# The operand that two comparison lines read lies in PSUM instead of SBUF, in a graph-network kernel

## The chip, the cores and the metric

The kernel runs on one core of one Trainium2 chip. The metric is the device time of that core in microseconds (us): the median of several executions.

## The reference

Four graph layers over 6250 nodes with 96 features each and 106250 edges, each followed by a residual sum and a layer norm. Cut to what matters here:

```
# layer 0, twice: an edge's message, the maximum over the edges that end in a node
msg = x[src] @ W_msg + edge_attr @ W_edge
agg = segment_max(msg, dst);  x' = leaky_relu(agg + x @ W_root + b)
# layer 1: weights from a small network on the edge, sum over the edges
agg = segment_sum(w(edge_attr) * x[src], dst)
# layer 2: two hops over the normalised adjacency; layer 3: one more
h = segment_sum(norm[:, None] * h[src], dst)
```

## The kernel before

**Two halves.** Layers 0 and 1 need x[src] for every edge: three passes over the edges (p = 0, 1, 2). Edges are sorted by destination and cut into 832 tiles of 128 edges; four tiles are a quarter (208 in a pass). Layers 2 and 3 are done with a dense adjacency matrix, 50 blocks of 128 nodes by 6272, which is counted up on the chip during passes 1 and 2 and written to memory, and then read and multiplied three times.

**The gathers.** GpSimd (POOL) issues one indirect DMA for each tile (line 851, `gath<-table,ids`), 832 in a pass, one after the other. It waits at a pass's start for the node table, and within a pass only that the work on the quarter eight back has let go of the buffer (`s_turn`, signalled by TensorE's line 1093; `s_msg` of VectorE's line 2343 in pass 2). A gather moves 128 rows of 384 bytes; its descriptors are made by software on GpSimd.

**A step of passes 0 and 1** works on one quarter. TensorE turns the gathered rows (L1090) and adds the edge's part (L1093); VectorE scans them (L2161, `scan`); TensorE turns back (L1107); VectorE makes the one-hots of the band (L2166); TensorE adds up (L1133). In pass 0 VectorE also makes the one-hots of a histogram (L1826, L1828): these compare with `span_ps`, a table of 0 to 127 as 4-byte numbers in PSUM bank 7. In pass 2 the step has a product (L2343) in place of the scan.

**The adjacency's windows.** In steps 8 to 207 of pass 1 and 0 to 199 of pass 2, VectorE builds one-hots for two windows of the adjacency: `window_hots` writes `hot_key` (128x392, bf16, L2190) and `hot_src` (128x128, bf16, L2192), two of each for a window, so four pairs a step and 1600 pairs in all. Each compares a table that is the same for all (`iota_key` of 392 int16 numbers, `iota_b` of 128 bf16 numbers, both in SBUF) with one number for each partition, a column of `key_t` in SBUF. TensorE multiplies them (L1161) into PSUM bank 6, and ScalarE takes the counts out (L1587). The window one-hots stand ahead of the same step's scan in VectorE's order; there are four buffers of each (`h`).

Every engine runs its instructions in the order written; semaphores join them. Between the test at the start (`falls_ps`) and the dense half, nothing but VectorE's `span_ps` is written to bank 7 in this path.

Of the kernel before, what the change touches and what calls it, by code (L numbers as in the profile page):

```python
# [24 lines left out]
BF16 = mybir.dt.bfloat16  # L25
I32 = mybir.dt.int32
I16 = mybir.dt.int16
ALU = mybir.AluOpType
# [7 lines left out]
P = 128  # L36
# [32 lines left out]
KEYS = HI * WINDOW  # L69
# [62 lines left out]
def gnn_kernel(nc, x_nodes, x_t, src_t, dst_t, dst_now, dst_before, ea17_t, ea32_t, ea17_rows, ea32_rows,  # L132
# [43 lines left out]
    with ctx:  # L176
        def sb(name, shape, dt=F32, at=None):
            return (at or ctx).enter_context(nc.sbuf_tensor(name, shape, dt))
# [42 lines left out]
        iota_b = sb("iota_b", [P, P], BF16)  # L221
        strays = sb("strays", [P, 2])
        rel_end = sb("rel_end", [P, TILES])
        iota_key = sb("iota_key", [P, KEYS], I16)
# [21 lines left out]
        with ExitStack() as sparse:  # L246
# [32 lines left out]
            with ExitStack() as of_fast:  # L279
# [4 lines left out]
                key_t = sb("key_t", [P, 2, KEY_TILES, NT * WINDOWS], at=of_fast)  # L284
# [5 lines left out]
                hot_key = sb("hot_key", [P, 4, KEY_TILES, KEYS], BF16, of_fast)  # L290
                hot_src = sb("hot_src", [P, 4, KEY_TILES, P], BF16, of_fast)
# [4 lines left out]
        banks = ctx.enter_context(nc.psum_tensor("banks", [P, 8, 512], F32))  # L296
# [22 lines left out]
        key_t_ps = [banks[:, b, 0:2 * KEY_TILES * GATHERED] for b in (6, 1)]  # L319
        window_ps = banks[:, 6, 0:KEYS]  # L320
        span_ps = banks[:, 7, 0:P]
        before_ps = banks[:, 0, 0:2 * NT]
        hid1_ps = banks[0:D, 0, :]
        wide_w_ps = [banks[:, b, 0:QT * D] for b in (4, 5)]
# [156 lines left out]
        def over_groups(eng, *stages):  # L481


            def step(i, b, known):
                for stage, lag in stages:
                    g = 2 * i + b - lag if known else None
                    if not known or 0 <= g < GROUPS:
                        stage(i + (b - lag) // 2, (b - lag) % 2, known and g < 2)
            for s in range(4):
                step(s // 2, s % 2, True)  # L490
            with eng.Fori(2, GPAIRS) as i:
                step(i, 0, False)
                step(i, 1, False)
            for s in range(GROUPS, GROUPS + max(lag for _, lag in stages)):
                step(s // 2, s % 2, True)
# [41 lines left out]
        def over_units(eng, peeled, *stages):  # L537

            def step(i, b, known):
                for stage, lag in stages:  # L540
                    t = 2 * i + b - lag if known else None
                    if not known or 0 <= t < UNITS:
                        stage(i + (b - lag) // 2, (b - lag) % 2, 1 if t == UNITS - 1 else 3)
            for s in range(peeled):
                step(s // 2, s % 2, True)
            with eng.Fori(peeled // 2, TRIOS // 2) as i:
                step(i, 0, False)
                step(i, 1, False)
            for s in range(TRIOS, UNITS + max(lag for _, lag in stages)):
                step(s // 2, s % 2, True)  # L550
# [1228 lines left out]
        def _(ve):  # L1779
# [353 lines left out]
            with ve.Else():  # L2133
# [3 lines left out]
                ve.tensor_tensor(rel_end[:, :], ids[:, 0, :], reaches()[:, 0:TILES], ALU.subtract)  # L2137
                ve.wait_ge(s_y[0], GROUPS)
                ve.tensor_copy(span_ps, iota_b[:, :])
                ve.wait_ge(s_next, 32)  # L2140
                ve.drain()
                ve.tensor_tensor(part[:, :].bitcast(F32), ids[:, 0, :], part[:, :], ALU.is_equal)
# [39 lines left out]
                def window_hots(p, i, k):  # L2182

                    for j in (0, 1):
                        n = WINDOWS * BUILT * (p - 1) + WINDOWS * i + 2 * k + j
                        h = 2 * (k % 2) + j
                        if n >= 4:
                            ve.wait_ge(s_window_mm, n - 3)
                        for a in range(KEY_TILES):
                            ve.tensor_scalar(hot_key[:, h, a, :], iota_key[:, :], key_t[:, 0, a, bass.ds(n, 1)],  # L2190
                                             None, ALU.is_equal)
                            last = ve.tensor_scalar(hot_src[:, h, a, :], iota_b[:, 0:P], key_t[:, 1, a, bass.ds(n, 1)],  # L2192
                                                    None, ALU.is_equal)
                        last.then_inc(s_window_hot, 1)

# [114 lines left out]
                for p in range(2):  # L2310
                    if p == 1:
                        degrees()
                        ve.wait_ge(s_x, 16)
                    for s in range(QUARTERS + TAIL):
                        for i, k in windows_at(p, s, 0):
                            window_hots(p, i, k)
                        if s < QUARTERS:
                            scan_quarter(p, s)
                        if 2 <= s < QUARTERS + 2:
                            hots_of_ends(p, s - 2)  # L2320
                        if p == 0 and s < QUARTERS:
                            one_hots(s)
                        for g in bands_at(p, s, 1):
                            rectify(p, g)
                        if p == 1:
                            for g in bands_at(p, s, 3):
                                add_rows(g)
                            for g in bands_at(p, s, 5):
                                factors_of(p, g)
                            if s == 2:  # L2330
                                key_places()
                        if s == KEYS_AT:
                            (make_keys if p == 0 else take_keys)()
# [16 lines left out]
                for s in range(QUARTERS + TAIL):  # L2350
                    if s + 1 < QUARTERS:
                        message(s + 1)
                    for i, k in windows_at(2, s, 0):
                        window_hots(2, i, k)
                    for g in bands_at(2, s, 2):
                        add_sums(g)
                    for g in bands_at(2, s, 4):
                        factors_of(2, g)
                    for g in bands_at(2, s, 6):
                        parts_of(g)  # L2360
# [111 lines left out]
```

## Time and profile before

| | us |
|---|---|
| median of 3 runs (4173.12 to 4182.38) | 4178.61 |
| the profiled execution, its time | 4181.7 |
| its span, first to last instruction | 4179.9 |
| PE busy | 3225.5 (77%) |
| POOL busy | 2408.2 (58%) |
| DVE busy | 2313.7 (55%) |
| ACT busy | 893.1 (21%) |

Engines: PE is TensorE, DVE VectorE, ACT ScalarE, POOL GpSimd. Busy shares are over the whole span, and they mix the gather passes (the first gather starts at 40.6 us, the last at 3255.4 us) with the dense half after them, in which POOL does nothing. In a row of groups, "x784 | 765.3, 976" is 784 instructions, 765.3 us busy together, 976 ns a piece; behind the next bar stands the idle time of the engine ahead of them, with what ended it. In a timeline row the first two numbers are start and duration in us.

### The profile page before, as it was taken

The page shows a single profiled execution, that of the slowest core. Times are in us where ns is not written, and L with a number is a line of the kernel's source. Part 1 is how long each engine was busy: PE and PEld are TensorE (multiplying, and loading weights), DVE is VectorE, ACT ScalarE, POOL GpSimd, SP SyncE. Part 2 cuts the span into 40 slices and gives each one's busy share as a digit, 9 for nine tenths or more (in the row PEclk, how much of TensorE's full clock was granted, in tenths as well). Part 3 has the DMA queues.
Part 4 walks back from the last instruction along what each step waited for, and adds up shares of the span by engine and source line. Part 5 has one row for each costly group of instructions (what it writes and reads, how often), then busy time and mean ns, then how long its engine had stood idle before and what let it go on. Part 6 is the DMA issues. An engine that isn't in the chain of part 4 may idle for free.

```text
span 4179.9 us, 64017 instructions
## 1 busy us (share of the span) xinstructions
PE 3225.5 (77%) x23472; PEld 2587.8 (62%) x23472; DVE 2313.7 (55%) x6280; ACT 893.1 (21%) x1914; POOL 2408.2 (58%) x2520
## 2 busy tenths in 40 slices
PE   3767666666667776777777778888778899999999
PEld 2545445555445454545545555555555899999999
DVE  3867677676567676767664565556655222223111
ACT  0111111111123232333333333333333000011011
POOL 4777777777677777777766777777777100000000
PEclk9888888898888898989898998889888899999999
DMA  5433333333344444444433333333333677777775
GB/s 154 120 84 73 84 84 75 83 73 86 68 110 115 118 114 120 108 120 110 118 89 89 101 89 93 88 93 90 99 93 83 225 268 268 266 271 263 263 260 208
DMA packets 173212, 555.29 MB, mean 133 GB/s; under 512 B 75512, under 2 KB 81115, under 8 KB 149146
## 3 DMA queue, kind: packets, MB, share of 16 engines
q1 hardware_dynamic: 62384, 335.45, 24.7%
q0 software_dynamic: 80432, 124.45, 14.3%
q10 hardware_dynamic: 30138, 92.02, 5.8%
q8 instruction: 153, 2.51, 0.3%
q14 instruction: 105, 0.86, 0.1%
HBM read 455.05 MB, written 96.37 MB: 132 GB/s over the span
## 4 chain that ended last, share of the span: by engine, by line
POOL 50%; PE 26%; issue 18%; DMA 4%; DVE 1%; ACTq 0%; ACT 0%; DVEq 0%; POOLq 0%; SPq 0%
POOL gath L851 50%; PE banks L1365 21%; DMA gath<-table,ids 2%; PE banks L1093 1%; DMA w_l<-in_w_l 1%; PE banks L1133 1%; PE banks L1090 1%; DMA gath<-in_dst_now 0%; PE banks L1107 0%; DMA key_got<-key_runs,key_ix 0%; PE banks L1161 0%; DVE hot_lo L1826 0%; DVE scan L2161 0%; PE banks L1349 0%; PE banks L877 0%
## 5 line engine op out<-in xcount | busy, mean ns | idle before, releaser
L851 POOL DMA_INDIRECT gath<-table,ids x2496 | 2396.9, 960 | 814.2 <-issue 750.2
L1365 PE MATMUL banks<-r_parts,adj_in 128*128 128x288 bf16 x7203 | 889.8, 286 | 6.9 <-DMA adj_in<-adjacency 5.7
L1365 PEld LDWEIGHTS banks<-r_parts,adj_in 128*128 128x128 bf16 x7203 | 883.2, 142 | 8.9 <-issue 5.9
L2161 DVE TENSOR_TENSOR_SCAN scan<-keep_of,scan,banks 96x512 f32<-96x512 bf16 x414 | 526.9, 1273 | 562.3 <-PE banks L1093 561.1
L1090 PE MATMUL banks<-ident,gath 128*96 128x128 f32 x1664 | 290.7, 303 | 634.6 <-issue 287.9
L1133 PE MATMUL banks<-back 128*96 128x104 f32 (+11 forms) x6000 | 688.3, 263 | 17.9 <-ACT back L1577 8.1
L1133 PEld LDWEIGHTS banks<-back 128*96 128x96 f32 x6000 | 648.5, 177 | 70.3 <-issue 41.3
L1090 PEld LDWEIGHTS banks<-ident,gath 128*96 128x96 f32 x1664 | 189.9, 137 | 700.3 <-issue 356.4
L1587 ACT ACTIVATE adj<-banks 128x392 bf16<-128x392 f32 x800 | 395.4, 494 | 1026.5 <-PE banks L1161 1024.6
L1161 PE MATMUL banks<-hot_key,hot_src 128*128 128x392 bf16 x1600 | 430.7, 353 | 215.0 <-DVE hot_src L2192 199.2
L2190 DVE TENSOR_SCALAR hot_key<-iota_key,key_t 128x392 bf16<-128x392 int16 x1600 | 546.7, 342 | 11.8 <-PE banks L1161 5.9
L1093 PE MATMUL banks<-ea_of,w_edge_of 128*96 128x512 f32 x832 | 493.5, 679 | 0.0
L1161 PEld LDWEIGHTS banks<-hot_key,hot_src 128*128 128x128 bf16 x1600 | 147.2, 105 | 528.9 <-DVE hot_src L2192 314.4
L2192 DVE TENSOR_SCALAR hot_src<-iota_b,key_t 128x128 bf16<-128x128 bf16 x1600 | 401.9, 251 | 0.0
L1577 ACT ACTIVATE back<-banks 128x384 f32<-128x384 f32 x416 | 203.1, 488 | 913.1 <-PE banks L1107 899.9
L2343 DVE TENSOR_TENSOR back<-banks,gath 128x384 f32<-128x384 f32 x208 | 115.5, 555 | 390.8 <-DMA gath<-table,ids 370.6
L1107 PEld LDWEIGHTS banks<-ident,scan 96*128 96x128 f32 x1664 | 208.4, 155 | 174.3 <-issue 151.8
L1300 PEld LDWEIGHTS banks<-w_edge_out,hid 97*128 97x128 f32 x1664 | 242.9, 214 | 28.8 <-issue 15.6
L2385 DVE TENSOR_REDUCE v<-banks 128x288 f32<-128x864 f32 (+1 forms) x34 | 34.8, 1022 | 404.1 <-PE banks L1365 404.0
L1300 PE MATMUL banks<-w_edge_out,hid 97*128 97x96 f32 x1664 | 241.2, 294 | 5.7 <-DVE back L2343 5.7
L1292 PE MATMUL banks<-ea_of,w_edge_of 128*96 128x512 f32 x416 | 236.5, 653 | 8.1 <-DMA ea_of<-in_ea_t 7.3
L2166 DVE TENSOR_TENSOR back<-rel_end,banks 128x416 f32<-128x416 f32 x416 | 231.7, 557 | 2.6 <-PE banks L1133 2.6
(167 smaller groups left out, 2042.5 us busy)
## 6 DMA issues: line engine op xcount, KB each, us to landing
adj_in<-adjacency SPq DMA_DIRECT2D x147, 1568.0 KB, 6.5
adjacency<-adj ACTq DMA_DIRECT2D x100, 784.0 KB, 5.8
gath<-table,ids POOLq DMA_INDIRECT x2496
ea_of<-in_ea_t SPq DMA_DIRECT2D x78, 512.0 KB
keep_of<-keep_max_d SPq DMA_DIRECT2D x52, 768.0 KB, 13.1
key_runs<-key_lines ACTq DMA_DIRECT2D x4, 896.0 KB
table<-x_sb SPq DMA_DIRECT2D x10, 240.0 KB, 4.3
back<-in_x_t SPq DMA_DIRECT2D x12, 192.0 KB
```

What stands on the lines that cost most here:

```text
L851: pool.indirect_dma_start(gath[:, b, t, :], None, tables[p][:, :], bass.IndirectOffsetOnAxis(ap=ids[:, 1, n:n + 1], axis=0),).then_inc(s_g ...
L1090: pe.matmul(turn_ps[q % 2][:, t * P:(t + 1) * P], gath[:, k // 4, QT * (k % 4) + t, :], ident[:, :], start=t == 0, stop=False, is_transpos ...
L1093: pe.matmul(turn_ps[q % 2], weights(p), columns, start=False, stop=True, skip_group_check=True).then_inc(s_turn, 1)
L1133: m = pe.matmul(band_ps[g % 2][:, at:at + n], rows_in[:, q % 2, t * D:(t + 1) * D], hot_dst[:, q % 2, t, first:first + n], start=False, st ...
L1161: m = pe.matmul(window_ps, hot_src[:, 2 * (k % 2) + j, a, :], hot_key[:, 2 * (k % 2) + j, a, :], start=a == 0, stop=a == KEY_TILES - 1)
L1292: pe.matmul(hid1_ps, weights(2), columns, start=True, stop=True).then_inc(s_hid_ps, 1)
L1300: m = pe.matmul(wide_w_ps[q % 2][:, t * D:(t + 1) * D], hid[:, q % 2, t * P:(t + 1) * P], W["edge_out"][:, :], start=True, stop=True)
L1365: m = pe.matmul(sum_ps[:, u, j, :], adj_in[:, a, :, h], r_parts[:, n % 2, h, :, :].rearrange("p k f -> p (k f)"), start=h == 0, stop=h == ...
L1587: act.activation(adj[:, half, at:at + WINDOW, :].rearrange("p d h -> p (d h)"), window_ps, ACT.Copy)\
L2161: ve.tensor_tensor_scan(scan[0:D, b, at:at + Q], keep_of[:, i % 2, CHUNK * b + at:CHUNK * b + at + Q], turn_ps[q % 2], start, ALU.min, ALU ...
L2190: ve.tensor_scalar(hot_key[:, h, a, :], iota_key[:, :], key_t[:, 0, a, bass.ds(n, 1)], None, ALU.is_equal)
L2192: last = ve.tensor_scalar(hot_src[:, h, a, :], iota_b[:, 0:P], key_t[:, 1, a, bass.ds(n, 1)], None, ALU.is_equal)
```

## The change

Two more tables in PSUM bank 7, behind `span_ps`: `key_places_ps`, the 392 int16 numbers of `iota_key`, and `src_places_ps`, the 128 bf16 numbers of `iota_b`. They are written once, as 4-byte words by a shift of 0 places (196 and 64 words). The two comparisons of `window_hots` read these in place of the tables in SBUF. Outputs, the numbers compared, counts and order stay.

```diff
+        key_places_ps = banks[:, 7, P:P + KEYS // 2].bitcast(I16)
+        src_places_ps = banks[:, 7, P + KEYS // 2:P + KEYS // 2 + P // 2].bitcast(BF16)
...
                 ve.tensor_copy(span_ps, iota_b[:, :])
+                ve.tensor_scalar(banks[:, 7, P:P + KEYS // 2].bitcast(I32), iota_key[:, :].bitcast(I32), 0, None, ALU.arith_shift_right)
+                ve.tensor_scalar(banks[:, 7, P + KEYS // 2:P + KEYS // 2 + P // 2].bitcast(I32), iota_b[:, :].bitcast(I32), 0, None, ALU.arith_shift_right)
                 ve.wait_ge(s_next, 32)
...
                         for a in range(KEY_TILES):
-                            ve.tensor_scalar(hot_key[:, h, a, :], iota_key[:, :], key_t[:, 0, a, bass.ds(n, 1)],
+                            ve.tensor_scalar(hot_key[:, h, a, :], key_places_ps, key_t[:, 0, a, bass.ds(n, 1)],
                                              None, ALU.is_equal)
-                            last = ve.tensor_scalar(hot_src[:, h, a, :], iota_b[:, 0:P], key_t[:, 1, a, bass.ds(n, 1)],
+                            last = ve.tensor_scalar(hot_src[:, h, a, :], src_places_ps, key_t[:, 1, a, bass.ds(n, 1)],
                                                     None, ALU.is_equal)
```

VectorE's queue with the change, at the end of its setup for the sparse half (`banks` is PSUM; `part` and `rel_end` are prepared for the band one-hots, and the first scan of pass 0 follows):

```order
L2139 TENSOR_TENSOR rel_end<-ids,agg 128x832
L2141 CAST banks<-iota_b 128x128
L2142 TENSOR_SCALAR banks<-iota_key 128x196
L2143 TENSOR_SCALAR banks<-iota_b 128x64
L2146 TENSOR_TENSOR part<-ids,part 128x832
L2148 SCALAR_TENSOR_TENSOR rel_end<-part,rel_end 128x832
L2165 SCALAR_TENSOR_TENSOR scan<-keep_of,banks 96x512
```

The rows of L2142 and L2143 are new there; they stand ahead of the wait for the row of `part`, and nothing else has moved (line numbers are four higher from there on). On no other engine does an instruction come, go or move.

## Rows read from the trace of the kernel before

**Rows 1.** The chain that ended last: shares of the span by engine.

```profile
POOL 50%; PE 26%; issue 18%; DMA 4%; DVE 1%; ACTq 0%; ACT 0%; DVEq 0%; POOLq 0%; SPq 0%
```

**Rows 2.** Busy us (instructions) in four stretches: PE, PEld, DVE, ACT, POOL; clock, DMA.

```profile
300.00:1090.00 790.00, 529.56 (x4436) 400.82 (x4437) 553.39 (x958) 86.88 (x176) 597.45 (x633) 0.86 0.34 78
1181.00:2184.20 1003.20, 728.66 (x4879) 508.63 (x4877) 703.83 (x2121) 310.82 (x693) 764.61 (x784) 0.90 0.42 113
2205.00:3225.10 1020.10, 801.07 (x4852) 575.61 (x4851) 602.79 (x2176) 359.20 (x715) 774.48 (x807) 0.88 0.33 92
3225.10:3256.40 31.30, 24.97 (x151) 20.48 (x150) 7.08 (x15) 4.30 (x8) 23.63 (x26) 0.76 0.26 65
```

**Rows 3.** POOL's groups: 300:1090, 1112:1181, 1181:2184.2, 2205:3225.1, 3225.1:3256.5, in this order.

```profile
L851 POOL DMA_INDIRECT gath<-table,ids x633 | 598.2, 945 | 192.9 <-issue 190.4 <-PE banks L1093 2.4
...
L851 POOL DMA_INDIRECT gath<-table,ids x49 | 46.3, 945 | 30.9 <-DMA table<-y 16.3 <-issue 14.3 <-DVE key_ix L2227 0.3
...
L851 POOL DMA_INDIRECT gath<-table,ids x784 | 765.3, 976 | 238.9 <-issue 235.5 <-PE banks L1093 3.4
...
L851 POOL DMA_INDIRECT gath<-table,ids x807 | 774.5, 960 | 266.4 <-issue 243.1 <-DMA table<-node 20.8 <-DVE back L2343 2.4
...
L851 POOL DMA_INDIRECT gath<-table,ids x26 | 24.6, 945 | 7.9 <-issue 7.9
```

**Rows 4.** Who POOL waited for, 1181:2184.2: us, times, longest.

```profile
POOL gath L851 <- issue: 235.5, 773, 0.3
```

**Rows 5.** Timeline of POOL and VectorE near the end of pass 1.

```profile
2180.65 0.94 POOL L851 DMA_INDIRECT gath<-table,ids  x1 [0.30 <-issue]
...
2181.16 0.52 DVE L2190 TENSOR_SCALAR hot_key<-iota_key,key_t 128x392 bf16<-128x392 int16 x1
...
2181.60 0.23 DVE L2192 TENSOR_SCALAR hot_src<-iota_b,key_t 128x128 bf16<-128x128 bf16 x1
...
2181.76 0.31 DVE L2190 TENSOR_SCALAR hot_key<-iota_key,key_t 128x392 bf16<-128x392 int16 x1
...
2181.90 1.07 POOL L851 DMA_INDIRECT gath<-table,ids  x1 [0.30 <-issue]
...
2183.28 0.94 POOL L851 DMA_INDIRECT gath<-table,ids  x1 [0.30 <-issue]
```

**Rows 6.** VectorE's groups of pass 0, 300:1090.

```profile
L2161 DVE TENSOR_TENSOR_SCAN scan<-keep_of,scan,banks 96x512 f32<-96x512 bf16 x159 | 202.4, 1273 | 221.2 <-PE banks L1093 221.0
L1826 DVE TENSOR_TENSOR hot_lo<-lo_dst,banks 128x512 bf16<-128x512 bf16 x158 | 107.2, 679 | 15.6 <-PE banks L1149 14.6 <-issue 0.4
```

**Rows 7.** VectorE's groups: two of 1181:2184.2 (pass 1), one of 2205:3225.1 (pass 2).

```profile
L2190 DVE TENSOR_SCALAR hot_key<-iota_key,key_t 128x392 bf16<-128x392 int16 x796 | 265.7, 334 | 11.8 <-PE banks L1161 5.9 <-ACT key_t L1610 5.5
L2161 DVE TENSOR_TENSOR_SCAN scan<-keep_of,scan,banks 96x512 f32<-96x512 bf16 x199 | 253.2, 1273 | 289.0 <-PE banks L1093 288.1
...
L1872 DVE CAST r_parts<-sq 128x384 bf16<-128x384 f32 x11 | 4.2, 379 | 0.8
```

**Rows 8.** Timeline of VectorE in pass 1: comparisons back to back.

```profile
1402.17 0.24 DVE L2192 TENSOR_SCALAR hot_src<-iota_b,key_t 128x128 bf16<-128x128 bf16 x1
1402.33 0.31 DVE L2190 TENSOR_SCALAR hot_key<-iota_key,key_t 128x392 bf16<-128x392 int16 x1
1402.56 0.31 DVE L2192 TENSOR_SCALAR hot_src<-iota_b,key_t 128x128 bf16<-128x128 bf16 x1
1402.72 0.31 DVE L2190 TENSOR_SCALAR hot_key<-iota_key,key_t 128x392 bf16<-128x392 int16 x1
```

**Rows 9.** Timeline of VectorE in pass 0: comparisons with the table in PSUM.

```profile
600.98 0.68 DVE L1826 TENSOR_TENSOR hot_lo<-lo_dst,banks 128x512 bf16<-128x512 bf16 x1
601.58 0.35 DVE L1828 TENSOR_TENSOR hot_hi<-hi_dst,banks 128x200 bf16<-128x200 bf16 x1
601.85 0.68 DVE L1826 TENSOR_TENSOR hot_lo<-lo_src,banks 128x512 bf16<-128x512 bf16 x1
```

**Rows 10.** Timeline of VectorE behind the place of the two new writes.

```profile
72.87 1.02 DVE L2142 TENSOR_TENSOR part<-ids,part 128x832 f32<-128x832 int32 x1 [26.54 <-DMA part<-ids]
```

## The prediction

> **What bounds the kernel now.** I read the chain that ended last first, then the busy times by stretch, then GpSimd's own groups in each stretch. The chain puts half of the span on POOL, and another 18% on "issue" [rows 1], which is time between instructions with nothing awaited. The only POOL work of any size is the gathers of L851, so the passes' length is their number times their period. That POOL is the bound, and not a queue that waits for others, is seen in what ended its idle time in pass 1: "issue" 235.5 us in 773 gaps, none over 0.3 us [rows 4]. Nobody holds it back there. Each gather is followed by a constant gap of 0.30 us [rows 5], and the next starts.
>
> So the question is how long one gather occupies POOL, and the groups by stretch answer it [rows 3]. In pass 0 a gather takes 945 ns (633 of them). At the start of pass 1, before the window one-hots begin, it takes 945. With the window one-hots running it takes 976 in pass 1 (784) and 960 in pass 2 (807). In pass 2's last steps, when they have ended, it takes 945 again. The same instruction, the same bytes, and its length changes exactly with the work of L2190 and L2192.
>
> The timeline shows how [rows 5]. The gather that starts at 2180.65 ends at 2181.59. A `hot_key` that starts inside it, at 2181.16, takes 0.52 us where 0.31 is usual, and so ends with the gather. The next gather starts at 2181.90, while a `hot_key` is under way, and takes 1.07 us where 0.94 is usual. Each makes the other wait: the two engines want something that only one can have at a time.
>
> Not every VectorE instruction does that. In pass 0 VectorE is busy 553 of 790 us [rows 2], as full as in pass 1 (704 of 1003), with scans and with one-hots that read `span_ps` in PSUM [rows 6], and the gathers stay at 945. These have one input in SBUF and one in PSUM; the scan even has a number per partition from SBUF besides.
>
> **The change part by part.**
>
> *The waiting of the gathers, removed.* Pass 1: 784 x (976 - 945) ns = 24.3 us. Pass 2: 807 x (960 - 945) ns = 12.1 us. From the second I take off what is not the comparisons' own: that stretch has 11 casts of L1872 [rows 7] and as many of L1868, SBUF to SBUF like the comparisons, and they will go on disturbing gathers. I estimate 0.1 us each, 2 us. That leaves 24 + 10 = 34 us. It goes straight to the end: POOL waits for nobody, pass 2 starts from pass 1's last gather, and the dense half starts from pass 2's.
>
> The whole 34 us is given back only if the comparisons no longer contend at all when their table lies in PSUM. The trace has no one-input comparison of 2-byte numbers in PSUM. The bounds are 0 (it contends as before) and 34 us. The nearest rows are those of pass 0 [rows 6], and they stand at no contention whatever: 945 ns. I take 34.
>
> The Trainium skill says the same as a mechanism. "SBUF — State Buffer", section "Who interferes with whom", has GpSimd share one pair of ports with VectorE as an exclusive lock that a `tensor_scalar` takes in its two-port modes, and descriptor making on GpSimd stands still meanwhile. "VectorE: DVE Perf Modes", section "Why PSUM operands drop a tier", has a PSUM operand exclude the two-port modes. The trace agrees with the first as far as it goes (0.52 and 1.07 us in rows 5); the second no run has shown yet.
>
> *The comparisons' own time, added.* Back to back, a `hot_key` holds the engine 0.23 us (1402.33 to 1402.56) and a `hot_src` 0.16 (1402.17 to 1402.33) [rows 8]: 0.07 us for 264 more numbers, 0.265 ns a number, and 0.13 us fixed. A pair takes 0.39. Comparisons with the PSUM table in pass 0 take 0.60 for 512 and 0.27 for 200 [rows 9]: 1.06 ns a number and 0.06 fixed. Those are two-input and read 4-byte numbers. What the new form costs is bounded from these:
> - least: half the present rate (0.53 ns a number) with the fixed part of rows 9: 0.06 + 0.21 and 0.06 + 0.07 = 0.40, nothing added;
> - most: the rate of rows 9 with the present fixed part: 0.13 + 0.42 and 0.13 + 0.14 = 0.82, that is +0.43 a pair;
> - taken: half the present rate and the present fixed part, 0.34 + 0.20 = 0.54, +0.15 a pair. The present rate is four times that of rows 9; no row lies between. I take the middle step because the inputs stay 2-byte numbers side by side, which those of rows 9 are not, while the memory becomes that of rows 9.
>
> Does that matter? VectorE has room: in pass 1 it idles 1003.2 - 703.8 = 299 us and in pass 2 417 us [rows 2]. Taken over 796 pairs, +0.15 is 119 us of the 299. The cover is the wait of the scan for TensorE, 289 us in that stretch [rows 7], which is a wait for gathers to land. Without that cover every pair would cost its 0.15 us, 240 us in all. A late scan delays POOL only once it is late by some seven quarters of 5 us, since the gathers run that far ahead. So: 0.
>
> The Trainium skill has a rule against this change. Its table in "VectorE: DVE Perf Modes", section on the TRN2 errata, charges 58 cycles fixed for an SBUF source and 120 for one in PSUM, at 0.96 GHz some 65 ns more per instruction, on top of the lower rate. That would make a pair 0.54 + 0.13 = 0.67 and add 223 of 299 us in pass 1: still hidden, the same time. The trace points the other way, a fixed 0.06 us with a PSUM operand against 0.13 [rows 8, 9].
>
> *The two writes, added.* At 196 and 64 words they cost under 0.6 us together by the rate and fixed part of rows 9. They stand ahead of a wait of 26.54 us for a transfer [rows 10]: hidden, 0. If that cover were gone: 0.6 us.
>
> *The tails.* When a pass's last gather lands, the engines run dry behind it. Pass 2 has no windows in its last eight steps. In pass 1 the last block of comparisons starts right behind a step's band one-hots and has the 4 us in which the gather is under way; 0.6 us more disappears in it.
>
> Sum: 4181.7 - 34 = 4147.7 for the profiled execution, which is 3.1 us above the median of the runs: 4178.6 - 34 = **4145 us**.
>
> **The rivals.**
>
> *A. It still contends.* The result still goes to SBUF and the number per partition still comes from there; if one of these is what is fought over, nothing changes: 4178.6. For it: no row has this very form. Against it: `hot_lo` writes 512 bf16 numbers to SBUF, the scan reads a number per partition, and pass 0 has 945 ns. Chance 0.08. A middle case, where the longer instruction contends on some of its way, gives half: 4162, chance 0.08.
>
> *B. VectorE becomes the bound (slower).* If the new form takes one number per clock as in rows 9 and keeps its fixed part, a pair takes 0.82. In pass 1 a step holds four pairs: VectorE's 703.8/199 = 3.54 us a step become 3.54 + 4 x 0.43 = 5.26, and a step lasts 5.04 now. Pass 1 would grow by 199 x 0.22 = 44 us, and pass 2, where VectorE has 417 us spare against 800 x 0.43 = 344, would still give 10: 4178.6 + 44 - 10 = 4213. It decides from +0.376 us a pair (299/796) on, and somewhat sooner as the scan's waits can't all be filled. For it: every PSUM row of the trace has that rate. Against it: they are all 4-byte and two-input. Chance 0.07.
>
> **How the numbers follow.** The forecast, the gathers back to 945 ns in both passes and VectorE hidden, has 0.77; with the executions' spread of some 5 us and the 2 us estimate its own range is 4138 to 4153. The middle case lies at 4153 to 4170, A at 4170 to 4187, B at 4190 to 4220. Leaving out A, B and the far part of the middle case leaves out less than 2 in 10: **4137 to 4165**. 0.2% is 8.4 us, about what a measurement of this kernel can tell from no change. Faster by more than that: 0.77 and most of the middle case, 0.84. Within it: 0.09. Slower: 0.07.
>
> **What would show it.** Right: the groups of L851 at 945 to 948 ns in pass 1 and about 947 in pass 2, the gaps still 0.30, the last gather starting some 34 us before 3255 us; `hot_key` no longer 0.52 anywhere beside a gather, pairs 0.5 to 0.6 us apart, VectorE's busy time in pass 1 up by about a tenth of the stretch. Wrong in the first step: gathers of 960 and 976 ns still there. Wrong in the second: POOL's idle time ended by PE L1093 or by a VectorE line with whole microseconds, and the scan's wait for PE gone. The dense half should not change: any difference behind the last gather is none of this argument.

## The result, and the profile after

The changed kernel takes 4143.59 us (median of 4 runs, 4141.57 to 4145.7), the kernel before 4180.49 beside it: a ratio of 0.9918, 95% interval 0.9906 to 0.993. That is 37 us less, at a forecast of 4145 and 34 less. Of the executions told of below, one was far slower than the others of its kernel (only `hot_src` from PSUM: 5133.3 us at a granted clock of 0.56 against 0.90) and is in no median and no ratio.

First the page's chain of waits of the changed kernel, then POOL's groups in the same five kinds of stretch as in [rows 3]: pass 0; pass 1 before the windows; pass 1 beside them; pass 2 beside them; the last steps of pass 2.

```profile
POOL 49%; PE 26%; issue 18%; DMA 4%; DVE 2%; SPq 0%; DVEq 0%; ACT 0%; ACTq 0%; POOLq 0%
```

```profile
L853 POOL DMA_INDIRECT gath<-table,ids x632 | 597.5, 945 | 192.6 <-issue 190.8 <-PE banks L1095 1.8
...
L853 POOL DMA_INDIRECT gath<-table,ids x47 | 44.4, 944 | 30.5 <-DMA table<-y 16.5 <-issue 14.0
...
L853 POOL DMA_INDIRECT gath<-table,ids x786 | 743.1, 945 | 239.5 <-issue 233.4 <-PE banks L1095 6.1
...
L853 POOL DMA_INDIRECT gath<-table,ids x808 | 764.0, 946 | 268.4 <-issue 242.9 <-DMA table<-node 22.4 <-DVE back L2347 3.0
...
L853 POOL DMA_INDIRECT gath<-table,ids x25 | 23.6, 943 | 7.6 <-issue 7.6
```

The third and fourth rows had 976 and 960 ns. Now every stretch has the 943 to 946 ns of a gather that nobody disturbs, and POOL is still the bound (49 + 18% of the chain). The gaps have not grown: 239.5 us for 786 gathers is 0.30 us each.

VectorE in pass 1 beside the windows, by groups, to be read beside [rows 7]; then the engines' busy us (PE, PEld, DVE, ACT, POOL) in four stretches, the last of them the dense half:

```profile
L2194 DVE TENSOR_SCALAR hot_key<-banks,key_t 128x392 bf16<-128x392 int16 x797 | 326.3, 409 | 12.1 <-PE banks L1163 6.5 <-ACT key_t L1612 5.4
L2165 DVE TENSOR_TENSOR_SCAN scan<-keep_of,scan,banks 96x512 f32<-96x512 bf16 x199 | 252.8, 1270 | 190.8 <-PE banks L1095 190.3
L2196 DVE TENSOR_SCALAR hot_src<-banks,key_t 128x128 bf16<-128x128 bf16 x796 | 216.3, 272 | 0.0
```

```profile
300.00:1090.00 790.00, 542.18 (x4464) 410.49 (x4465) 553.84 (x957) 87.17 (x176) 597.38 (x632) 0.84 0.34 78
1174.00:2156.70 982.70, 739.89 (x4891) 518.96 (x4890) 781.51 (x2123) 312.52 (x693) 742.60 (x786) 0.88 0.43 115
2179.20:3187.80 1008.60, 791.61 (x4854) 569.27 (x4854) 673.45 (x2178) 360.77 (x715) 762.67 (x808) 0.89 0.33 93
3219.00:4141.80 922.80, 903.84 (x7360) 900.96 (x7360) 211.90 (x597) 76.21 (x211) 0.00 (x0) 0.99 0.72 259
```

VectorE works longer for the same result (781.5 us in a stretch that is 20 us shorter, where it was 703.8), and pays with idle time: the scan's wait for PE fell from 289 to 190 us. The last gather's stretch ends at 3219.0 us where it ended at 3256.4, 37 us earlier, and the dense half takes its 923 us as before (4179.9 - 3256.4 = 923.5).

A piece of the timeline, POOL and VectorE in pass 1, shows what no longer happens:

```profile
1395.84 0.94 POOL L853 DMA_INDIRECT gath<-table,ids  x1 [0.30 <-issue]
1395.91 0.41 DVE L2194 TENSOR_SCALAR hot_key<-banks,key_t 128x392 bf16<-128x392 int16 x1
1396.24 0.27 DVE L2196 TENSOR_SCALAR hot_src<-banks,key_t 128x128 bf16<-128x128 bf16 x1
1396.43 0.41 DVE L2194 TENSOR_SCALAR hot_key<-banks,key_t 128x392 bf16<-128x392 int16 x1
1396.76 0.27 DVE L2196 TENSOR_SCALAR hot_src<-banks,key_t 128x128 bf16<-128x128 bf16 x1
1396.95 0.41 DVE L2194 TENSOR_SCALAR hot_key<-banks,key_t 128x392 bf16<-128x392 int16 x1
1397.08 0.94 POOL L853 DMA_INDIRECT gath<-table,ids  x1 [0.30 <-issue]
```

Comparisons start at different moments of a gather, and neither is longer for it. They also give the new form's price: 0.33 us for `hot_key` (1396.43 to 1396.76) and 0.19 for `hot_src` (1396.24 to 1396.43). That is 0.14 us for 264 numbers, 0.53 ns a number, and 0.12 us fixed, where [rows 8] gave 0.13.

### The profile page after: what moved, and what is told of

Read it like the earlier page. It is cut to its first block, busy times and chain, and to the rows that moved or that the text cites. A ratio compares the mean times of both kernels' runs of the same rounds, so it can differ in the third digit from the quotient of the medians.

```text
span 4141.8 us, 64019 instructions
## 1 busy us (share of the span) xinstructions
PE 3235.8 (78%) x23472; PEld 2597.4 (63%) x23472; DVE 2460.8 (59%) x6282; ACT 895.3 (22%) x1914; POOL 2373.2 (57%) x2520
## 4 chain that ended last, share of the span: by engine, by line
POOL 49%; PE 26%; issue 18%; DMA 4%; DVE 2%; SPq 0%; DVEq 0%; ACT 0%; ACTq 0%; POOLq 0%
POOL gath L853 49%; PE banks L1367 21%; DMA gath<-table,ids 3%; PE banks L1095 1%; PE banks L1135 1%; PE banks L1092 1%; DMA ea_of<-in_ea_t 1%; PE banks L1163 1%; DMA gath<-in_dst_now 0%; PE banks L1109 0%; PE banks L1351 0%; SPq L681 0%; DVE hot_key L2194 0%; DVE back L2347 0%; POOL key_got L863 0%
## 5 line engine op out<-in xcount | busy, mean ns | idle before, releaser
L853 POOL DMA_INDIRECT gath<-table,ids x2496 | 2361.9, 946 | 811.5 <-issue 748.2
L2194 DVE TENSOR_SCALAR hot_key<-banks,key_t 128x392 bf16<-128x392 int16 x1600 | 656.8, 411 | 12.1 <-PE banks L1163 6.5
L2196 DVE TENSOR_SCALAR hot_src<-banks,key_t 128x128 bf16<-128x128 bf16 x1600 | 436.8, 273 | 0.0
L1109 PE MATMUL banks<-ident,scan 96*128 96x96 f32 x1664 | 231.6, 267 | 3.9 <-ACT back L1579 3.9
```

The source lines that it names most:

```text
L853: pool.indirect_dma_start(gath[:, b, t, :], None, tables[p][:, :], bass.IndirectOffsetOnAxis(ap=ids[:, 1, n:n + 1], axis=0),).then_inc(s_g ...
L1109: m = pe.transpose(back1_ps[:, t * D:(t + 1) * D], scan[0:D, k // 4, at + t * P:at + (t + 1) * P], ident[0:D, 0:D])
L2194: ve.tensor_scalar(hot_key[:, h, a, :], key_places_ps, key_t[:, 0, a, bass.ds(n, 1)], None, ALU.is_equal)
L2196: last = ve.tensor_scalar(hot_src[:, h, a, :], src_places_ps, key_t[:, 1, a, bass.ds(n, 1)], None, ALU.is_equal)
```

## The experiments

Twelve experiments ran on eleven kernels (the drain alone twice); three of them, on another chip, are told of further down only. Each ratio is to the kernel before as it ran beside (medians of 4177 to 4180 us). The last two columns are the mean length of a gather beside the windows, from POOL's groups.

| kernel | us | ratio to before, 95% | pass 1, ns | pass 2, ns |
|---|---|---|---|---|
| before [rows 3] | 4179 | | 976 | 960 |
| changed | 4143.6 | 0.9906 to 0.993 | 945 | 946 |
| only hot_key from PSUM | 4148.8 | 0.9906 to 0.994 | 947 | 947 |
| only hot_src from PSUM | 4171.1 | 0.9973 to 0.9992 | 963 | 961 |
| 4-byte tables in SBUF | 4178.1 | 0.9988 to 1.0007 | 982 | 954 |
| changed, histogram from SBUF | 4322.7 | 1.0313 to 1.0358 | 947 | 947 |
| changed, all comparisons twice | 4496.4 | 1.0741 to 1.0787 | 945 | 944 |
| changed, hot_src twice | 4151.0 | 0.9916 to 0.9954 | 947 | 947 |
| changed, hot_key twice | 4239.0 | 1.0132 to 1.0169 | 948 | 947 |
| before, hot_key twice, drain | 4158.5 | 0.9943 to 0.9973 | 952 | 954 |
| before, drain alone | 4164.5 | 0.9959 to 0.998 | 956 | 957 |

### Each part alone

```diff
# e1: only hot_key reads PSUM
-  last = ve.tensor_scalar(hot_src[:, h, a, :], src_places_ps, key_t[:, 1, a, bass.ds(n, 1)], ...
+  last = ve.tensor_scalar(hot_src[:, h, a, :], iota_b[:, 0:P], key_t[:, 1, a, bass.ds(n, 1)], ...
# e2: only hot_src reads PSUM
-  ve.tensor_scalar(hot_key[:, h, a, :], key_places_ps, key_t[:, 0, a, bass.ds(n, 1)], ...
+  ve.tensor_scalar(hot_key[:, h, a, :], iota_key[:, :], key_t[:, 0, a, bass.ds(n, 1)], ...
```

> One part alone: hot_key reads its table from PSUM, hot_src still from SBUF. Theory (a one-input comparison that runs SBUF to SBUF and a gather's descriptor making keep each other waiting, each for as long as the other holds): hot_key no longer disturbs, hot_src does as before. It is the shorter of the two (0.16 us of a pair's 0.39), so a third or less of the 31 and 15 ns stays: gathers of some 955 ns in pass 1 and 949 in pass 2, the whole about 4155 us. Rival (each VectorE instruction that reads a table in SBUF costs the same, whatever its length): half stays, 960 and 953 ns, about 4162 us. Rival (only VectorE's total load counts): no step at all between the two kernels, since the load rose with the change.

> The other part alone: hot_src from PSUM, hot_key from SBUF. Theory: the longer instruction still disturbs, two thirds or more of the excess stay: 967 ns or more in pass 1, 955 or more in pass 2, about 4168 us. Rival of equal shares: 960 and 953 ns, 4162 us. Together with the run before, the savings of the two should add to about 36 us if they act independently.

POOL's groups beside the windows of pass 1 and of pass 2, with only `hot_key` in PSUM:

```profile
L853 POOL DMA_INDIRECT gath<-table,ids x786 | 744.1, 947 | 239.5 <-issue 234.4 <-PE banks L1095 5.2
...
L853 POOL DMA_INDIRECT gath<-table,ids x807 | 763.9, 947 | 266.4 <-issue 243.8 <-DMA table<-node 20.8 <-DVE back L2347 1.8
```

and with only `hot_src` in PSUM:

```profile
L853 POOL DMA_INDIRECT gath<-table,ids x786 | 756.8, 963 | 239.6 <-issue 234.4 <-PE banks L1095 5.2
...
L853 POOL DMA_INDIRECT gath<-table,ids x808 | 776.2, 961 | 266.7 <-issue 244.4 <-DMA table<-node 20.8 <-DVE back L2347 1.5
```

`hot_key` carries nearly all: 30 us of the 36 come with it alone, 8 with `hot_src` alone. In the two profiled executions 5.5 us of what separates "only hot_key" from the changed kernel lie ahead of pass 1 (its first gather starts at 1113.0 us against 1107.5), so the gathers are the better measure: 947 ns against 945 and 946. Equal shares per instruction are out, and so is the idea that VectorE's load sets it. My third for `hot_src` alone was too much (947 ns measured in both passes, 955 and 949 expected). Nor do the shares add up pass by pass: with only `hot_src` moved, pass 1 fell from 976 to 963 ns, further than the 967 or more that I had expected, and pass 2 did not fall at all.

### The same length of comparison, the other memory

```diff
# before, with the tables as 4-byte numbers in SBUF
+  ve.tensor_copy(wide_tables[:, 0:KEYS], iota_key[:, :])
+  ve.tensor_copy(wide_tables[:, KEYS:KEYS + P], iota_b[:, :])
...
-  ve.tensor_scalar(hot_key[:, h, a, :], iota_key[:, :], key_t[:, 0, a, bass.ds(n, 1)], ...
+  ve.tensor_scalar(hot_key[:, h, a, :], wide_tables[:, 0:KEYS], key_t[:, 0, a, bass.ds(n, 1)], ...
```

(`hot_src` likewise.)

> Both tables stay in SBUF but as 4-byte numbers, so that a comparison should take as long as with the PSUM table (hot_key 0.33 us and hot_src 0.19 us start to start) and VectorE's load is that of the changed kernel; only the memory differs. Theory (the place of the input decides): the gathers stay disturbed, and somewhat more than before as the comparisons last longer: 976 ns or up to 990 in pass 1, 960 to 970 in pass 2, the whole 4178 to 4195 us. Rival (it is the fast form, four 2-byte numbers a cycle, that disturbs, and any slower form would have done): gathers back to 945 ns, the whole about 4144 us.

POOL beside the windows of pass 1 and of pass 2; then the durations (least, median, most, in ns) of `hot_key` in this kernel and in the changed one:

```profile
L853 POOL DMA_INDIRECT gath<-table,ids x784 | 770.0, 982 | 238.9 <-issue 234.7 <-PE banks L1095 4.3
...
L853 POOL DMA_INDIRECT gath<-table,ids x808 | 770.7, 954 | 268.4 <-issue 242.9 <-DMA table<-node 22.4 <-DVE back L2349 3.0
```

```profile
L2192 DVE TENSOR_SCALAR hot_key<-agg,key_t x1600: 389/414/651, 1177.2 to 3223.6; 128x392 bf16<-128x392 f32 x178
```

```profile
L2194 DVE TENSOR_SCALAR hot_key<-banks,key_t x1600: 386/411/423, 1174.0 to 3186.9; 128x392 bf16<-128x392 int16 x178
```

This is the cleanest pair of the study. The median `hot_key` takes the same time in both (414 and 411 ns), yet from SBUF it is held up to 651 ns and the gathers are lengthened about as in the kernel before, 4178.1 us in all; from PSUM nothing passes 423, and the gathers are at 945. Between these two the memory of the input decides, not the speed of the comparison. My amounts held for pass 1 (982 ns) and not for pass 2: 954 ns, where I had expected 960 to 970 and the kernel before has 960, so a longer comparison from SBUF need not disturb more. A one-input comparison from SBUF that takes more than 0.53 ns a number was not run.

### Two inputs in SBUF

```diff
# changed kernel, pass 0's histogram one-hots
-  quarter_hots("dst", q % 2, q, 0, span_ps)
-  quarter_hots("src", q % 2, q, 1, span_ps).then_inc(s_hot, 1)
+  quarter_hots("dst", q % 2, q, 0)          # iota_b, in SBUF
+  quarter_hots("src", q % 2, q, 1).then_inc(s_hot, 1)
```

> The changed kernel, with the four histogram one-hots of each pass 0 step reading their table (iota_b) from SBUF in place of PSUM: two inputs in SBUF. Passes 1 and 2 as in the changed kernel (946 ns). Theory A (two inputs in SBUF contend too, since the gather reads its indices from there): pass 0 gathers go over 945 ns, by an amount that no row gives; the few two-input SBUF instructions of node_t in pass 0 lengthened 6 of the 15 gathers beside them by 0.24 us, which over 832 gathers would be some 80 us, the whole up to 4225 us. Theory B (only the one-input form contends): pass 0 stays at 945 ns, the whole at 4144 us.

POOL's and one of VectorE's groups in pass 0, 300:1250; then a piece of the timeline:

```profile
L853 POOL DMA_INDIRECT gath<-table,ids x652 | 753.2, 1155 | 198.7 <-issue 197.2 <-PE banks L1095 1.5
```

```profile
L1828 DVE TENSOR_TENSOR hot_lo<-lo_src,iota_b 128x512 bf16<-128x512 bf16 x164 | 111.7, 681 | 0.0
```

```profile
604.14 2.88 POOL L853 DMA_INDIRECT gath<-table,ids  x1 [0.31 <-issue]
604.37 0.68 DVE L1828 TENSOR_TENSOR hot_lo<-lo_dst,iota_b 128x512 bf16<-128x512 bf16 x1
604.97 0.35 DVE L1830 TENSOR_TENSOR hot_hi<-hi_dst,iota_b 128x200 bf16<-128x200 bf16 x1
605.25 0.68 DVE L1828 TENSOR_TENSOR hot_lo<-lo_src,iota_b 128x512 bf16<-128x512 bf16 x1
605.85 0.35 DVE L1830 TENSOR_TENSOR hot_hi<-hi_src,iota_b 128x200 bf16<-128x200 bf16 x1
```

Much more than I had expected: 179 us over the changed kernel, where I had thought of 80 at most. The gather from 604.14 lasts 2.88 us, over the whole block of four comparisons, which ends at about 606.2, and then finishes. It does not happen to every gather: in this trace 595 of pass 0's 832 are within 5 ns of 944, and 220 take over 1 us, the longest 4.22. VectorE is hardly held up (`hot_lo` 681 and 685 ns on average, against 677 to 679 from PSUM). So this contention is nearly one-sided, and back-to-back instructions can keep a gather waiting to their end. Passes 1 and 2, untouched, stay at 947 ns. The Trainium skill, "SBUF — State Buffer", section "Who interferes with whom", states that a VectorE instruction with two SBUF inputs contends with a GpSimd instruction that reads SBUF; the trace agrees, 1155 ns against 945.

### When the cover is gone

```diff
# changed kernel, hot_key twice (a second time into unused SBUF); src twice, and both twice, likewise
 def window_hots(p, i, k):
+  ve.drain()
...
+  ve.tensor_scalar(spare_key[:, (2 * j + a) * KEYS:(2 * j + a + 1) * KEYS], key_places_ps, key_t[:, 0, a, bass.ds(n, 1)], ...
   ve.tensor_scalar(hot_key[:, h, a, :], key_places_ps, key_t[:, 0, a, bass.ds(n, 1)], ...
```

> The changed kernel with every window comparison done twice from PSUM (the extra results go to unused SBUF and a drain of VectorE stands ahead of each block). The cost of the comparisons is hidden only while VectorE has room: in pass 1 of the changed kernel it is busy 781.5 of 982.7 us beside the windows, in pass 2 673 of 1008. Twice adds 0.521 us a pair. Theory (PSUM comparisons leave the gathers alone, and cost nothing up to VectorE's room): gathers stay at 946 ns, but POOL now waits for PE, pass 1 grows by 781.5 + 415 - 982.7 = 214 us or more, pass 2 by 673 + 417 - 1008 = 82 or more: 4440 us or more. Rival (there is much more slack, since VectorE's busy time counts overlaps): clearly less than 4400.

> The changed kernel with only hot_src done twice from PSUM: +0.191 us a pair, 152 us of the 201 free in pass 1. Theory (hidden up to the room, which is 0.25 us a pair in pass 1): gathers at 946 ns, POOL waits for nobody in pass 1, the whole within 5 us of the changed kernel's 4144. Rival (room can't be used to the end, since the scans' waits for gathers fall where they fall): POOL's waits for PE L1095 appear in pass 1 and the whole grows by 10 us or more.

> The changed kernel with only hot_key done twice from PSUM: +0.329 us a pair, just over the 0.25 that pass 1 has free. Theory: gathers at 946 ns, pass 1 longer by 781.5 + 262 - 982.7 = 61 us or a little more with the drains, pass 2 (673 + 264 of 1008) no longer: about 4205 to 4225 us. Rival (more room than the busy time tells): no longer than 4160.

POOL beside pass 1's windows, with `hot_src` twice, with `hot_key` twice, and with both twice:

```profile
L856 POOL DMA_INDIRECT gath<-table,ids x784 | 742.2, 947 | 238.9 <-issue 233.4 <-PE banks L1098 5.5
```

```profile
L855 POOL DMA_INDIRECT gath<-table,ids x783 | 742.2, 948 | 296.7 <-issue 226.6 <-PE banks L1097 70.1
```

```profile
L856 POOL DMA_INDIRECT gath<-table,ids x785 | 741.8, 945 | 442.1 <-PE banks L1098 234.4 <-issue 207.7
```

The gathers stay at 945 to 948 ns, also under twice the PSUM comparisons, so what is left is pure VectorE time. +0.19 us a pair is hidden in pass 1, where POOL waits 5.5 us for PE, as in the changed kernel (6.1). The whole, 4151.0, is 7 us above the changed kernel's, neither within the 5 that I expected nor the rival's 10; in the profiled executions 5.6 us of the difference lie ahead of pass 1 (its first gather at 1113.1 us against 1107.5), where no comparison was doubled. +0.33 is not hidden: POOL now waits 70 us for PE in pass 1, where I had expected 61 and a little for the drains. The whole grew by 95 us, more than my 61 to 81, because the backlog also delays pass 2's table (POOL's wait for it is 56.4 us against 22.4). +0.52 costs 353 us, with 214 + 82 as the floor. So the threshold lies between 0.19 and 0.33 us a pair, on either side of the 0.25 that the free time gave; the change used 0.13 of the 0.376 that were free before.

### A surprise: more comparisons from SBUF, and less disturbance

```diff
# before, hot_key twice from SBUF, with the drain
+  ve.drain()
...
+  ve.tensor_scalar(spare_key[:, (2 * j + a) * KEYS:(2 * j + a + 1) * KEYS], iota_key[:, :], key_t[:, 0, a, bass.ds(n, 1)], ...
# before, the drain alone
+  ve.drain()
```

> The kernel before with hot_key done twice from SBUF: +0.232 us a pair, 185 of the 299 us free in pass 1, so VectorE itself stays hidden. Theory (each hot_key from SBUF disturbs the gathers by itself, about 18 ns a gather in pass 1 and 11 in pass 2 each): gathers of some 995 ns in pass 1 and 970 in pass 2 and the whole 20 to 35 us longer, 4200 to 4215. Rival (a gather is disturbed once by a block of comparisons, however long it is): 4179 us as before.

It came out some 20 us *faster* than before, at 4158.5, where I had expected 20 to 35 slower. Neither theory held. Two readings were left, the drain or the moments, and three kernels were to part them:

> The kernel before with nothing but a drain of VectorE ahead of each block of window comparisons, as the kernel with hot_key twice had it (which came out at 4158 us, 20 us faster than before, against my expectation of 4200 to 4215). Theory (what a block costs a gather is set by the moments in the gather at which its comparisons start, so extra work can lower it as well as raise it): a drain moves a block by less than 0.1 us and leaves its inner cadence of 0.39 us a pair, so gathers keep a mean excess like before's, 15 to 35 ns in pass 1: 4165 to 4185 us. Rival (the drain itself parts the two-input instruction from the comparisons and so removes the disturbance): 950 ns or so, about 4155 us, as in the kernel with hot_key twice.

> The kernel before with hot_src (not hot_key) twice from SBUF, and the drain: a cadence of 0.55 us for the three instead of 0.39 for two or 0.63 for three with hot_key twice. Theory (the moments decide): some other mean excess, not given by the number of comparisons; it can be anything from a few ns to 50, and the gathers' phases should recur as in the others. Rival (each comparison from SBUF costs its own share): more than before, over 976 and 960 ns, over 4180 us. Rival (the drain): about 4155 us.

> The kernel before with the same comparisons in another order inside a window: both hot_key, then both hot_src, instead of in turns. Same instructions, same VectorE time, no drain. Theory (the moments decide): the mean excess of the gathers changes by more than 5 ns in one of the passes at least, and the whole by 5 us or more either way. Rival (the amount of comparing from SBUF decides): 976 and 960 ns, 4179 us.

These three ran on a chip that took 4874.2 us for the kernel before, and gave 4881.1, 4893.3 and 4877.4 us. POOL's waits in the first of them, 1505 us in all:

```profile
POOL gath L851 <- issue: 686.6, 2175, 1.6
POOL gath L851 <- remote: 330.4, 166, 8.0
POOL gath L851 <- DVE back L2344: 272.3, 93, 7.8
POOL gath L851 <- PE banks L1093: 130.5, 59, 11.5
```

POOL is not the bound there, so their times tell nothing about the gathers. Their gathers took 955 to 962 ns on average in each of passes 1 and 2, but no trace of the kernel before from that chip stands beside them. What slowed that chip I don't know. The drain alone was run once more:

> The kernel before with only the drain ahead of each block of window comparisons, once more: in the run before this the chip executed the kernel before in 4874 us instead of 4178, with waits all over the engines and POOL no longer the bound, so its three kernels say little about the gathers. Same theories: the moments decide, a mean excess of 15 to 35 ns in pass 1 and 4165 to 4185 us; or the drain is what lowered the disturbance in the kernel with hot_key twice, some 950 ns and 4155 us.

POOL beside the windows of pass 1 and of pass 2, and a piece of its timeline:

```profile
L851 POOL DMA_INDIRECT gath<-table,ids x785 | 750.1, 956 | 239.2 <-issue 235.3 <-PE banks L1093 4.0
...
L851 POOL DMA_INDIRECT gath<-table,ids x807 | 772.6, 957 | 268.1 <-issue 243.8 <-DMA table<-node 22.5 <-DVE back L2344 1.8
```

```profile
1506.10 0.94 POOL L851 DMA_INDIRECT gath<-table,ids  x1 [0.30 <-issue]
1506.62 0.52 DVE L2191 TENSOR_SCALAR hot_key<-iota_key,key_t 128x392 bf16<-128x392 int16 x1
...
1507.35 0.99 POOL L851 DMA_INDIRECT gath<-table,ids  x1 [0.30 <-issue]
1507.44 0.24 DVE L2193 TENSOR_SCALAR hot_src<-iota_b,key_t 128x128 bf16<-128x128 bf16 x1
1507.60 0.31 DVE L2191 TENSOR_SCALAR hot_key<-iota_key,key_t 128x392 bf16<-128x392 int16 x1
...
1508.00 0.42 DVE L2191 TENSOR_SCALAR hot_key<-iota_key,key_t 128x392 bf16<-128x392 int16 x1
```

The drain alone takes 12 us off (4164.5), with the same comparisons from SBUF. Neither of its two expectations was met: the mean excess in pass 1 is 11 ns, below the 15 to 35 of the one and above the 5 of the other. So a part of the surprise is the drain, and the rest (956 to 952 ns in pass 1, 957 to 954 in pass 2) comes with twice the `hot_key`s. The drain does not remove the disturbance.

The timeline suggests why amounts don't add up. A `hot_key` that starts 0.52 us into a gather is held; a `hot_src` and a `hot_key` that start 0.09 and 0.25 us into the next are not; the `hot_key` 0.65 into it is held again, for less, and that gather is 0.05 us longer.

The whole trace of the kernel before says the same. The durations (least, median, most, in ns) of its `hot_key`s, and of its gathers beside the windows of pass 1:

```profile
L2190 DVE TENSOR_SCALAR hot_key<-iota_key,key_t x1600: 286/311/556, 1180.8 to 3224.8; 128x392 bf16<-128x392 int16 x178
```

```profile
L851 POOL DMA_INDIRECT gath<-table,ids x784: 940/945/1524, 1180.3 to 2183.3; - x196
```

Of its 1600 `hot_key`s 367 are more than 40 ns over the median of 311, and 364 of these start 0.45 to 0.85 us into a gather. Of the 1664 gathers of passes 1 and 2 three quarters (1225) are within 5 ns of 944. Some find comparisons running at their start and still 0.2 us later: 458, which are 68 ns too long on average and carry 31 of the 38 us that all together lose. The other 1206 are 6 ns too long. In the changed kernel 659 gathers start into running comparisons in this way, and they are not longer (-0.4 ns on average). So a block that is under way when a gather starts can make the gather wait, and a comparison that starts in the gather's later part can be made to wait by it. With the drain alone 500 gathers start into a block, more than before, but they are only 36 ns too long. What halves that is open. That finer moments are the cause is argued, and not isolated by a run: the kernel that changed the order alone met the slow chip.

## Why the prediction was right

*POOL is the bound, and a gather's length is the term.* Right. 784 x 31 ns and 807 x 15 ns, less 2 us, were to come back. In the profiles the two stretches gave 786 x 31 = 24 us and 808 x 14 = 11 us. My 2 us for the casts was about 1 too much: pass 2's gathers are at 946, not 947. Of the 1664 gathers of passes 1 and 2 only 15 are still more than 20 ns too long, and each has beside it a VectorE instruction whose inputs all lie in SBUF (`node_t`, `sq`, `v`, `key_got`). The remaining 3 us of the 38 between the two profiled executions are not the gathers' length: pass 1's first gather starts 4.2 us sooner (1107.5 us against 1111.7), while POOL waits 1.6 us longer for pass 2's table and the dense half is 0.7 us shorter. Executions of one kernel differ by more, so that 37 us came and not 34 is no finding.

*The new form doesn't contend.* This was taken from pass 0's rows, which are of two-input instructions on 4-byte numbers. It held for the one-input form too, and the pair of SBUF against PSUM at equal speed shows that it is the input's memory. That step went beyond its rows; the prediction had put 0.16 on the cases in which something still contends. Rival A (the result's or the number's place in SBUF) is out: both stayed there.

*The comparisons' own time.* Taken +0.15 us a pair, measured 0.52 - 0.39 = +0.13. The rate is 0.53 ns a number, half as fast as before, and the fixed part is nearly the same. The Trainium skill, "VectorE: DVE Perf Modes", section "Why PSUM operands drop a tier", has PSUM cap 2-byte numbers at two a cycle; the trace agrees with 0.53 ns. The surcharge for a PSUM source that the Trainium skill has ("VectorE: DVE Perf Modes", section on the TRN2 errata: 120 cycles fixed against 58, an estimated 65 ns at 0.96 GHz) does not show in this trace: 0.12 us fixed from PSUM, 0.13 from SBUF.

*Hidden.* Right, and for the reason given: the scan's wait for PE shrank by 98 us in pass 1. Rival B did not come, since the new form has twice the rate of rows 9's. Its threshold of +0.376 us a pair stands near where it was put: doubling `hot_src` in the changed kernel makes +0.32 over the kernel before and stays hidden, doubling `hot_key` makes +0.46 and costs 95 us.

*The two writes.* They took 0.35 and 0.22 us at 46 us, in front of a wait for `part` that ended at 76.0. They cost nothing.

## What to carry to other kernels

Where software-made DMAs on GpSimd are the bound, sort their mean length by stretch against what VectorE does in it: an instruction that grows from 945 to 976 ns without a change of its own points to something shared. Then move an operand of VectorE's concurrent instructions to PSUM, even at half their speed, as long as VectorE has idle time that waits for the very gathers. Two-input instructions with both operands in SBUF are the first to look for; here four short ones a step cost 179 us. How much it brings is not to be had from the number of such instructions (below); a run has to say.

## What the runs showed that was not expected

Two SBUF inputs can block a gather until a whole run of such instructions is over (2.88 us for 0.94), while VectorE feels next to nothing (3 to 6 ns on average). One SBUF input, in a comparison at 0.27 or 0.53 ns a number, is mutual: in the kernel before four in five of the lengthened gathers took up to 1.07 us, and a comparison took up to 0.56 for 0.31. But here too a block can keep a gather waiting: the longest took 1.52 us. The cost of this second kind is no function of its amount: 4158.5 us with 1600 more such comparisons and a drain, 4164.5 with the drain alone, 4179 with neither. No experiment gave a version better than the changed kernel.
